# Perceiver block on one core: key rows before the latents, the key bias written by ScalarE, key-scale reciprocals on GpSimd

## The chip, the cores and the metric

The kernel runs on one core of a Trainium2 chip. The metric is the device time of one execution in microseconds. The engines of a core are TensorE (PE in the profile, its weight loads PEld), VectorE (DVE), ScalarE (ACT), GpSimd (POOL) and the DMA queue of SyncE (SP). Three runs of the kernel before took 455.82, 457.80 and 461.06 us, so its median is 457.8 us.

## The reference

Two layers are applied to `x` (2 x 128 x 256) with a context of 2 x 2048 rows of 256. What the change touches is the first layer's state-space block and the key half of the second layer's cross-attention:

```python
# layer 0, first part: multi-head latent attention, x += MLA(...)
# layer 0, second part (state-space block)
xz = x @ W_in.T ; xc = silu(conv(xp)) ; delta = softplus(dt @ W_dt.T + b_dt)
h = exp(delta*A[n]) * h + delta*B[n]*xc        # a scan over 128 positions, 16 states n
y = (sum_n h*C[n] + xc*Dp) * silu(z)           # the sum over n
# layer 1, cross-attention, from the context alone
k = ctx @ Wk + bk                              # 4096 rows x 256
s = max(abs(k), per row and head of 16)/127, at least 1e-8
kq = round(k / s) * s                          # 8-bit keys, one scale per row and head
v = ctx @ Wv + bv                              # per-channel scale from max(abs(v))
```

## The kernel before, in words

All loads, instructions and semaphores are written out by hand: each engine has its own program, run strictly in the order in which it is written, and a `wait_ge` on a semaphore holds everything behind it on that engine. One buffer `arena` holds most tiles at hand-set offsets; `w` in the trace is the tile `w1` with the state-space weights and, at its end, the key and value projection `w_kv` and its bias. `ps` is the eight accumulator banks.

The program has four stages that matter here.

**Latent attention (to about 78 us).** TensorE computes scores, turns the probabilities over (`prob_columns`, L1578), multiplies them with gathered latents (`weighted_latents`, L1591; `kvg` comes by nine DMAs) and projects them out (`attended`, L1598), once for each of the two batches b. In between stands `keys(0)` (L1633 and L1639), which needs `w1` to be loaded; SyncE issues that whole load after the nine gathers.

**State-space preparation (78 to 104 us).** Layer norm, projections, convolution, delta. VectorE's `first_input` (L1242) waits for the skip term's matmuls (`skip_read`).

**The loop (104 to 192 us).** Eight steps i, each with two of the sixteen states (s = 0, 1), interleaved with the key and value projection of 512 context rows per step. VectorE per step: two scans (L1251), two products with C (`read_out`, L1260), and for the keys two steps on `key_maxima` (L1150), the reciprocal of their scales (L1155) and `scaled_keys` (L1158), then `largest` of the values (L1187). GpSimd makes the scan inputs (L646) and the scales (L616). ScalarE makes decays (L906), evicts values (L830) and rounds the keys (`integers`, L838 and L841). TensorE per step: `key_columns` (L1659), `values_of` (L1648), the sums over states (L1748), `read_rows` (L1740), and `keys(i+3)`. Keys from step 1 on use only banks 2 and 3, so `keys(i+3)` waits until `scaled_keys(i+2)` has read them (`k_scaled`). The bias of the keys is the first matmul of each accumulation: a row of ones times the bias split into three bf16 parts (L1633), one for each bank.

**Values, feed-forward, queries, attention (from 192 us).** The 8-bit values are turned over (`value_rows`, L1836), the queries are made (L1822, L1335 to L1341), turned over (L1844) and masked by head (L691), and from 222 us VectorE reads scores (`maxima`, L1358), 32 units of four chunks, with `head_scales(h)` loading each head's key scales by DMA.

Of the kernel before, what the change touches and what calls it, by code (L numbers as in the profile page):

```python
# [14 lines left out]
P = 128  # L15
# [54 lines left out]
SUMS_PE = (0, 1, 2, 3, 4, 5, 6)  # L70
# [24 lines left out]
def perceiver_kernel(nc, x_d, seg_d, segrep_d, ctx_d, ctxT_d, rope_d, cst_d, w0a_d, w0q_d, w0b_d, w1_d, w2_d, w3_d, fill_d, out_d):  # L95
    with ExitStack() as ctx:
# [26 lines left out]
        neghalf = sb("neghalf", [P, B])  # L123
        spare = sb("spare", [P, 1])
# [95 lines left out]
        a_log = part(ET * DS).rearrange("p (t s) -> p t s", t=ET)  # L220
        w_kv = part(CH * 2 * D).rearrange("p (c n) -> p c n", c=CH)
# [41 lines left out]
        phase(2 * KEYS)  # L263
        vqb = take([CH, KEYS], BF16)
# [75 lines left out]
        (QLAT, WABS, MLAT, LAST_TAPS, DLAT, DLIN0, DLIN1, DBC, B_ROWS, Q_PS0, Q_PS1, Q_TR0, Q_TR1, ON_TR0, ON_TR1, VALUE0_MADE, Q_MADE,  # L340
# [16 lines left out]
        ld_w1 = sem("ld_w1")  # L357
        kvm_ready = sem("kvm_ready")
# [7 lines left out]
        k_scaled = sem("k_scaled")  # L366
        kmx_made = sem("kmx_made")
        ksc_made = sem("ksc_made")
        skip_read = sem("skip_read")
# [14 lines left out]
        qz_pool = sem("qz_pool")  # L384
        s_read = sem("s_read")
# [85 lines left out]
        rsum = sem("rsum")  # L471
# [30 lines left out]
        def _(sp):  # L502
# [21 lines left out]
            key_rows(1)  # L524
            sp.wait_ge(st_kv, 32)
# [3 lines left out]
            sp.dma_start(w1[:, :], w1_d).then_inc(ld_w1, 16)  # L529
# [44 lines left out]
        def _(pool):  # L574
# [3 lines left out]
            pool.wait_ge(half, 3)  # L578
# [20 lines left out]
            pool.wait_ge(ld_w1, 16)  # L599
# [49 lines left out]
            def sum_of(i):  # L649

                pool.wait_ge(hc_made, 2 * i + 2)
                pool.wait_ge(hc_used[1], i + 1)
                pool.tensor_tensor(th[:, :], th[:, :],
                                   hc[:, 1].rearrange("p t n -> p (t n)"), ALU.add).then_inc(hc_used[1], 1)

            pool.wait_ge(delta_ready, 2)
            pool.memset(th[:, :], 0.0).then_inc(hc_used[1], 1)
            pool.wait_ge(u_ready, 1)
            for i in range(NC - 1):
# [4 lines left out]
                if i not in SUMS_PE:  # L664
                    sum_of(i)
# [23 lines left out]
            for b in range(B):  # L689
                pool.wait_ge(qT_sb, b + 1)  # L690
                pool.tensor_scalar(qz[0][:, 0, b * L:(b + 1) * L], qT2[:, 0, b * L:(b + 1) * L], hmask[:, 0:1], None, ALU.mult)\  # L691
                    .then_inc(qz_pool, 1)
# [17 lines left out]
        def _(act):  # L710
# [103 lines left out]
            for b in range(B):  # L814
                act.activation(kvg[0:1, b * GB:(b + 1) * GB, :], bank(7, b * KVC, KVC, 0, 1).unsqueeze(1)
# [26 lines left out]

            def key_columns(i):
# [8 lines left out]
            key_columns(0)  # L852
            act.wait_ge(ld_w1, 16)
# [62 lines left out]
            for i in range(NC - 1):  # L916
# [3 lines left out]
                for m in range(CH):  # L920
                    values_of(i + 1, m)
                if i + 2 < NC:
# [114 lines left out]
        def _(dve):  # L1037
# [114 lines left out]
            def scaled_keys(i):  # L1152

                dve.wait_ge(ksc_made, i + 1)
# [975 lines left out]
```

## Time and profile before

| what | value |
|---|---|
| median of three runs | 457.8 us |
| the profiled execution's own time | 456.92 us |
| its span, first to last instruction | 454.7 us |
| busy: PE / DVE / ACT / POOL | 410.1 / 363.9 / 308.8 / 105.9 us |
| mean granted TensorE clock | 0.985 |

The profile shows one execution. Its time is 2.2 us above its span, which is what lies outside the first and last instruction. The longest chain of waits is made of TensorE for 43% and of VectorE for 35%. A busy share is a mean over stages: TensorE's 90% holds idle stretches, and in the loop it is close to 100%.

### The profile page before, as it was taken

The numbers are of one execution on the slowest core, as the hardware profiler recorded it, in microseconds if no ns is written. First come the engines' busy times: TensorE is split into PE (matmuls) and PEld (weight loads), VectorE is DVE, ScalarE is ACT, GpSimd is POOL, SyncE is SP. The second block draws the span as 40 slices with busy tenths as digits, with TensorE's granted clock in tenths as the row PEclk, the third lists the DMA queues.
The fourth block names the chain that finished last, engine by engine and source line by source line (L and its number), as shares of the span: only waits on it lengthen the run. The fifth ranks groups of instructions, "written<-read, shape, count | busy, mean of one in ns | idle before, by whom it ended". The sixth has DMA issues, their size and how long they took to land.

```text
span 454.7 us, 9348 instructions
## 1 busy us (share of the span) xinstructions
PE 410.1 (90%) x3814; PEld 308.5 (68%) x3854; DVE 363.9 (80%) x593; ACT 308.8 (68%) x394; POOL 105.9 (23%) x180
## 2 busy tenths in 40 slices
PE   8989889999999999799859889899888888888897
PEld 4778667865566554367527777777777777775586
DVE  2936643688999999888889999999999999955442
ACT  3256915579666667352888999999999999951120
POOL 4100030223555444000236333331111111100000
PEclk9999969999999999899989999999999999999999
DMA  7897920601100100079293554444444444000000
GB/s 273 291 398 250 189 119 1 255 3 46 25 23 27 32 14 0 0 255 438 106 368 140 196 219 190 190 187 186 187 186 186 187 188 186 3 1 0 2 0 23
DMA packets 13060, 63.32 MB, mean 139 GB/s; under 512 B 5946, under 2 KB 8666, under 8 KB 9562
## 3 DMA queue, kind: packets, MB, share of 16 engines
q1 hardware_dynamic: 12442, 59.19, 35.2%
q0 software_dynamic: 576, 3.54, 2.1%
q8 instruction: 30, 0.49, 0.4%
q14 instruction: 12, 0.10, 0.1%
HBM read 61.58 MB, written 1.15 MB: 138 GB/s over the span
## 4 chain that ended last, share of the span: by engine, by line
PE 43%; DVE 35%; issue 9%; DMA 7%; ACT 3%; SPq 2%; POOL 1%; DVEq 0%; POOLq 0%; ACTq 0%
DVE arena L1358 16%; DVE w L1358 8%; PE ps L1648 6%; PE ps L1748 6%; PE ps L1639 5%; DVE arena L1368 4%; PE ps L2014 3%; DMA w<-in_w 3%; PE ps L1534 2%; DMA arena<-in_segg 2%; PE ps L1688 2%; DMA arena<-ks_scr 2%; PE ps L2025 2%; DMA kv_scr<-arena 1%; PE ps L1890 1%
## 5 line engine op out<-in xcount | busy, mean ns | idle before, releaser
L1358 DVE CUSTOM_DVE_ANT_0 arena<-ps,arena 128x1024 f32<-128x1024 f32 x88 | 108.3, 1281 | 0.0
L1867 PE MATMUL ps<-arena 128*128 128x512 bf16 x216 | 68.2, 382 | 21.7 <-DVE arena L1358 18.5
L977 ACT ACTIVATE arena<-arena 128x4096 uint8<-128x4096 f32 x21 | 78.0, 3713 | 4.1 <-POOL arena L682 4.0
L1890 PEld LDWEIGHTS ps<-cst,arena 128*128 128x128 f32 x512 | 63.4, 141 | 24.8 <-issue 0.9
L1890 PE MATMUL ps<-cst,arena 128*128 128x128 f32 x512 | 77.3, 274 | 0.8 <-ACT arena L991 0.8
L1903 PE MATMUL ps<-vrow,arena 128*128 128x16 f16 x1024 | 59.7, 169 | 0.7 <-DVE arena L1368 0.6
L1903 PEld LDWEIGHTS ps<-vrow,arena 128*128 128x128 f16 x1024 | 53.2, 97 | 2.6 <-DVE arena L1368 1.3
L1358 DVE CUSTOM_DVE_ANT_0 w<-ps,arena 128x1024 f32<-128x1024 f32 x40 | 49.7, 1281 | 2.3 <-DMA arena<-ks_scr 2.3
L991 ACT ACTIVATE arena<-ps 128x512 f32<-128x512 f32 x91 | 47.4, 587 | 3.7 <-PE ps L1890 3.7
L1902 PE MATMUL ps<-vrow,arena 128*128 128x16 f16 x728 | 47.6, 170 | 0.2 <-ACT arena L991 0.2
L1902 PEld LDWEIGHTS ps<-vrow,arena 128*128 128x128 f16 x728 | 44.9, 96 | 0.3 <-ACT arena L991 0.3
L646 POOL TENSOR_TENSOR arena<-arena 128x1024 f32<-128x1024 f32 x14 | 33.0, 2361 | 40.2 <-DVE arena L1251 40.2
L678 POOL TENSOR_SCALAR arena<-arena 128x1 f32<-128x1 f32 x32 | 11.8, 369 | 121.3 <-DVE arena L1358 121.2
L977 ACT ACTIVATE arena<-w,arena 128x4096 uint8<-128x4096 f32 x10 | 37.1, 3714 | 2.0 <-POOL arena L682 2.0
L1251 DVE TENSOR_TENSOR_SCAN arena<-arena 128x1024 f32<-128x1024 f32 x16 | 37.2, 2363 | 0.2
L1748 PE MATMUL ps<-arena,cst 128*128 128x512 f32 x64 | 30.9, 624 | 2.5 <-DVE arena L1260 2.5
L906 ACT ACTIVATE arena<-arena 128x254 f32<-128x254 f32 x64 | 27.1, 495 | 5.8 <-DVE arena L1251 4.2
L1867 PEld LDWEIGHTS ps<-arena 128*128 128x128 bf16 x256 | 15.8, 96 | 22.3 <-issue 15.6
L1639 PE MATMUL ps<-w,arena 128*128 128x256 f32 x128 | 30.2, 379 | 0.0
L1648 PE MATMUL ps<-arena,w 128*128 128x512 f32 x64 | 29.4, 600 | 0.0
L1368 DVE TENSOR_SCALAR arena<-ps 128x1024 f16<-128x1024 f16 x37 | 25.4, 689 | 3.0 <-PE ps L1903 1.7
L1639 PEld LDWEIGHTS ps<-w,arena 128*128 128x128 f32 x128 | 24.3, 189 | 4.4 <-issue 0.3
(271 smaller groups left out, 694.5 us busy)
## 6 DMA issues: line engine op xcount, KB each, us to landing
arena<-ks_scr SPq DMA_DIRECT2D x16, 2048.0 KB, 7.6
arena<-in_w SPq DMA_DIRECT2D x1, 4488.0 KB, 17.3
arena<-in_columns SPq DMA_DIRECT2D x4, 1024.0 KB, 9.0
w<-in_w SPq DMA_DIRECT2D x1, 2927.0 KB, 12.9
arena<-in_w0b SPq DMA_DIRECT2D x1, 2560.0 KB, 18.5
arena<-in_w SPq DMA_DIRECT2D x1, 2048.0 KB, 7.9
arena<-in_fill SPq DMA_DIRECT2D x1, 2048.0 KB, 8.2
arena<-bc_scr SPq DMA_DIRECT2D x14, 128.0 KB, 3.1
```

Of the source, the lines that this page charges most:

```text
L977: act.activation(out8[:, :, 0], s_sb[u % 3], ACT.Exp, bias=nb[:, u % 3:u % 3 + 1], accum_out=zall[:, u:u + 1]).then_inc(p_ready, 1)
L991: act.activation(ptr[:, c, :].bitcast(F32), bank(4 + n % 3, 0, 512), ACT.Copy).then_inc(ptr_sb[1], 1)
L1251: dve.tensor_tensor_scan(hst[:, s, :], dA[:, s].rearrange("p t n -> p (t n)"), dbx[:, s].rearrange("p t n -> p (t n)"), 0.0, ALU.mult, ALU ...
L1358: dve.tensor_tensor_reduce(s_sb[slot][:, keys], ps[:, 2 * (c % 2):2 * (c % 2) + 2, :].rearrange("p a n -> p (a n)"), ksb[h % 2][:, keys], ...
L1368: dve.tensor_scalar(ptr[:, c, :], bank(4 + n % 3, 0, 512).bitcast(F16), -1024.0, None, ALU.add).then_inc(ptr_sb[0], 1)
L1639: mm = pe.matmul(bank(k_at + a, t * D, D), vT[:, c, i * CK + k:i * CK + k + P], w_kv[:, c, 0:D], start=False, stop=(c == CH - 1), skip_gro ...
L1648: mm = pe.matmul(bank(m, 0, CK), w_kv[:, c, D + m * P:D + (m + 1) * P], vT[:, c, i * CK:(i + 1) * CK], start=(c == 0), stop=(c == CH - 1))
L1748: mm = pe.matmul(bank(6 + n, 0, 512), ident, rows[:, n * 512:(n + 1) * 512], start=False, stop=True, skip_group_check=True)
L1867: mm = pe.matmul(bank(2 * (c % 2) + m, 0, 512), qz[h // 8][:, h % 8, b * L:(b + 1) * L], kT[:, h // 8, k:k + 512], start=True, stop=True)
L1890: mm = pe.transpose(bank(4 + n % 3, k * P, P), words[:, w:w + P], ident)
L1902: pe.matmul(bank(7, u * HW, HW), neg1024[:, :], vrow[:, h // 2, v:v + HW], start=False, stop=False)
L1903: mm = pe.matmul(bank(7, u * HW, HW), ptr[:, c, k * 2 * P + par:(k + 1) * 2 * P:2], vrow[:, h // 2, v:v + HW], start=(t == 0), stop=(t == ...
```

## The change

Eight edits, with no other line touched.

1. `w1` is loaded in two parts. The part from `w_kv` on goes first, ahead of the nine gathers, with its own semaphore `ld_wkv`. `keys(0)` moves on TensorE ahead of `weighted_latents(0)`, and on VectorE `key_maxima(0)` and `scaled_keys(0)` move ahead of the first residual. The row of means goes to bank 1 instead of 7.
2. `first_input` no longer waits for `skip_read`; the first `read_out` does.
3. From `keys(2)` on there is no bias matmul. ScalarE writes the bias into banks 2 and 3 (`key_bias`), after `k_scaled`, and TensorE waits for that (`bias_set`).
4. The reciprocals move from VectorE to GpSimd, as a power of -1 in one instruction behind each `scales_of` (`krs_made`).
5. VectorE reads `largest(i)` between `read_out(i, 1)` and `scaled_keys(i+2)`, no longer after it.
6. The clearing of `th` and its sum (two matmuls of zeros at the loop's end) go; 18 matmuls into an unused bank (`awake(18, 1)`) come before the last sums, once the values are evicted.
7. The integer values `vqb` lie in `w1`, so `head_scales(1)` is issued right behind `head_scales(0)`; VectorE's third unit waits for `vr_tr` instead.
8. On TensorE `value_rows(2)` and `query_columns(0)` come ahead of `queries(1)`, in place of `awake(2)`; head 0's masked queries are made by ScalarE (`q_first`), not GpSimd.

```diff
@@ SyncE
             key_rows(1)
+            sp.dma_start(w1[:, kv_at:W1], w1_d[:, kv_at:W1]).then_inc(ld_wkv, 16)
             sp.wait_ge(st_kv, 32)
...
-            sp.dma_start(w1[:, :], w1_d).then_inc(ld_w1, 16)
+            sp.dma_start(w1[:, 0:kv_at], w1_d[:, 0:kv_at]).then_inc(ld_w1, 16)
...
             head_scales(0)
+            head_scales(1)
             sp.wait_ge(vq_ready, 4)
             sp.dma_start(w3b, w3_d[:, w3a:W3]).then_inc(ld_w3b, 16)
-            sp.wait_ge(vr_tr, 8)
-            head_scales(1)
@@ GpSimd, scales_of(i)
                     .then_inc(ksc_made, 1)
+                pool.wait_ge(ksc_made, i + 1)
+                if i:
+                    pool.wait_ge(k_scaled, i)
+                pool.tensor_tensor(krs[:, :], ksc[:, i * CT * H:(i + 1) * CT * H], negone[:, :], ALU.pow).then_inc(krs_made, 1)
...
-            pool.memset(th[:, :], 0.0).then_inc(hc_used[1], 1)
@@ ScalarE
+            def key_bias(i):
+                act.wait_ge(k_scaled, i)
+                act.activation(ps[:, 2:4, :].rearrange("p a (t d) -> p (a t) d", d=D),
+                               b_k[:, :].unsqueeze(1).broadcast_to([P, CT, D]), ACT.Copy).then_inc(bias_set, 1)
...
                 for m in range(CH):
                     values_of(i + 1, m)
+                if i + 3 < NC:
+                    key_bias(i + 3)
                 if i + 2 < NC:
                     integers(i + 2)
...
             def query_columns(b):
                 act.wait_ge(pe_step, (Q_TR0, Q_TR1)[b])
+                act.activation(qz[0][:, 0, b * L:(b + 1) * L], bank((4, 7)[b], 0, L // 2).bitcast(BF16), ACT.Identity,
+                               scale=hmask[:, 0:1]).then_inc(q_first, 1)
@@ VectorE
             def scaled_keys(i):
-                dve.wait_ge(ksc_made, i + 1)
-                link(dve.reciprocal(krs[:, :], ksc[:, i * CT * H:(i + 1) * CT * H]))
+                dve.wait_ge(krs_made, i + 1)
...
-            dve.wait_ge(skip_read, 1)
             dve.wait_ge(z_gate, 1)
...
                 read_out(i, 1)
+                largest(i)
                 if i + 2 < NC:
                     scaled_keys(i + 2)
-                largest(i)
@@ TensorE
             def keys(i):
                 if i > 1:
-                    pe.wait_ge(k_scaled, i)
+                    pe.wait_ge(bias_set, i - 1)
...
-                    pe.matmul(bank(k_at + a, 0, 2 * D), selb[0:S3, 0:1].broadcast_to([S3, P]), ...
+                    if i < 2:
+                        pe.matmul(bank(k_at + a, 0, 2 * D), selb[0:S3, 0:1].broadcast_to([S3, P]), ...
...
-            pe.wait_ge(hc_used[1], NC)
-            sum_of(NC - 2, 1, th)
-            first_sum(NC - 1)
+            pe.wait_ge(v_sb, CH * NC)
+            awake(18, 1)
+            sum_of(NC - 1, 0)
...
             columns(3, 1)
-            awake(2, 0)
+            value_rows(2)
+            query_columns(0)
             queries(1)
-            query_columns(0)
-            value_rows(2)
```

On VectorE, step 0 of the loop and the scans of step 1, before. Here `ps` is the banks and `arena` everything in the big buffer; the instruction named SCALAR_TENSOR_TENSOR on L1251 is the scan.

```order
L1260 TENSOR_TENSOR arena<-arena,ps 128x1024 [waits c_ps,h_ready]
L1150 TENSOR_REDUCE arena<-ps 128x64 [waits ksc_made,k_ps]
L1260 TENSOR_TENSOR arena<-arena,ps 128x1024 [waits c_ps,h_ready]
L1155 RECIPROCAL arena<-arena 128x64 [waits ksc_made]
L1158 TENSOR_TENSOR arena<-ps,arena 128x1024 [waits kint_ready,dve_chain]
L1187 TENSOR_REDUCE arena<-arena 128x2 [waits v_sb]
L1251 SCALAR_TENSOR_TENSOR arena<-arena 128x1024 [waits dbx_ready,dA_ready,hc_made] x2
```

The same place in the change; L1266 is `read_out`, L1156 `key_maxima`, L1192 `largest`, L1163 `scaled_keys`.

```order
L1266 TENSOR_TENSOR arena<-arena,ps 128x1024 [waits c_ps,skip_read,h_ready]
L1156 TENSOR_REDUCE arena<-ps 128x64 [waits ksc_made,k_ps]
L1266 TENSOR_TENSOR arena<-arena,ps 128x1024 [waits c_ps,h_ready]
L1192 TENSOR_REDUCE arena<-arena 128x2 [waits v_sb]
L1163 TENSOR_TENSOR arena<-ps,arena 128x1024 [waits kint_ready,krs_made]
L1255 SCALAR_TENSOR_TENSOR arena<-arena 128x1024 [waits dbx_ready,dA_ready,hc_made] x2
```

The reciprocal has gone from the row, and `largest` stands between the second `read_out` and `scaled_keys`.

On GpSimd, one step of the loop in the change. L654 is a scan input, L620 the scales, and L625, which before has no counterpart, the power.

```order
L654 TENSOR_TENSOR arena<-arena 128x1024 [waits h_ready,ld_b0]
L620 TENSOR_SCALAR arena<-arena 128x64 [waits kmx_made]
L625 TENSOR_TENSOR arena<-arena,negone 128x64 [waits k_scaled,ksc_made]
L654 TENSOR_TENSOR arena<-arena 128x1024 [waits h_ready,ld_b1]
```

The power stands between the two scan inputs of the step, so the second of them starts later by its length.

On TensorE, the end of the latent attention's first half, in the change. L1586 is `prob_columns`, L1643 and L1649 `keys(0)`, L1599 `weighted_latents`, L1606 `attended(0)`.

```order
L1586 MATMUL ps<-cst,vrow 73x128 [waits pt_sb,probs]
L1586 MATMUL ps<-cst,vrow 73x128 x3
L1643 MATMUL ps<-arena,selb 128x512 [waits ld_wkv,bk3_ready,wvo_sb]
L1649 MATMUL ps<-w,arena 128x256 x4
L1643 MATMUL ps<-arena,selb 128x512
L1649 MATMUL ps<-w,arena 128x256 x4
L1599 MATMUL ps<-arena 64x64 [waits kvm_ready,pt_sb,ld_kvg]
L1599 MATMUL ps<-arena 64x64 x15
L1599 MATMUL ps<-arena 64x64 [waits kvm_ready,pt_sb]
L1599 MATMUL ps<-arena 64x64 x15
L1606 MATMUL ps<-arena 128x256 [waits ot_sb]
L1606 MATMUL ps<-arena 128x256 x7
```

Before, the four rows of `keys(0)` stood behind those of `attended(0)`, with waits for `ld_w1` and `kvm_ready` besides.

## Rows read from the trace of the kernel before

**Rows 1.** Windows: start:end, length, busy us of PE, PEld, DVE, ACT, POOL, clock, DMA

```profile
58.00:65.00 7.00, 6.74 (x16) 5.02 (x16) 2.43 (x5) 0.10 (x1) 2.50 (x5) 0.55 0.25 104
234.00:400.00 166.00, 148.34 (x2354) 124.97 (x2393) 164.18 (x273) 159.32 (x151) 41.62 (x107) 0.99 0.45 177
```

**Rows 2.** Timeline, 53 to 84 us: start, us, engine, line, tiles, idle before

```profile
55.20 2.09 PE L1591 MATMUL ps<-arena 73*64 73x64 f32 x64 [1.08 <-DMA arena<-kv_scr]
...
58.15 6.74 PE L1598 MATMUL ps<-arena 128*128 128x256 f32 x16 [0.87 <-ACT arena L808]
...
62.16 0.39 POOL L601 CAST arena<-w 96x256 bf16<-96x256 f32 x1 [48.87 <-DMA w<-in_w]
...
65.66 0.38 PE L1633 MATMUL ps<-arena,selb 96*128 96x512 bf16 x1 [0.77 <-POOL arena L610]
...
69.55 1.04 PE L1578 MATMUL ps<-cst,vrow 128*73 128x128 f32 x8
...
74.75 3.72 PE L1598 MATMUL ps<-arena 128*128 128x256 f32 x16 [0.70 <-ACT arena L808]
```

**Rows 3.** Timeline, preparation and the loop's first VectorE work

```profile
86.93 4.15 DVE L1197 SCALAR_TENSOR_TENSOR arena<-arena,w 128x256 f32<-128x256 f32 x9 [0.72 <-ACT arena L862]
...
101.31 1.30 DVE L1234 TENSOR_TENSOR arena<-arena 128x1024 f32<-128x1024 f32 x1
...
104.58 1.22 DVE L1242 TENSOR_TENSOR arena<-arena,ps 128x1024 f32<-128x1024 f32 x1 [1.97 <-PE ps L1730]
```

**Rows 4.** The chain of waits: keys(3), both halves, and keys(7)

```profile
117.55 1.73 PE ps L1639 x8
119.49 1.73 PE ps L1639 x8
...
163.47 1.73 PE ps L1639 x8
```

**Rows 5.** Timeline, step 3 of the loop, VectorE and ScalarE

```profile
144.53 1.22 DVE L1150 TENSOR_REDUCE arena<-ps 128x64 f32<-128x1024 f32 x1
145.66 1.21 DVE L1260 TENSOR_TENSOR arena<-arena,ps 128x1024 f32<-128x1024 f32 x1
146.79 0.55 DVE L1155 RECIPROCAL arena<-arena 128x64 f32<-128x64 f32 x1
147.37 1.23 DVE L1158 TENSOR_TENSOR arena<-ps,arena 128x1024 f32<-128x1024 f32 x1
...
149.31 1.15 ACT L838 ACTIVATE arena<-arena,cst 128x1024 f32<-128x1024 f32 x1
...
149.64 4.46 DVE L1251 TENSOR_TENSOR_SCAN arena<-arena 128x1024 f32<-128x1024 f32 x2
```

**Rows 6.** Groups of POOL instructions over the whole span, busy us and mean ns

```profile
L678 POOL TENSOR_SCALAR arena<-arena 128x1 f32<-128x1 f32 x32 | 11.8, 369 | 121.3 <-DVE arena L1358 121.2
...
L583 POOL TENSOR_TENSOR ln_rs<-ln_ve,neghalf 128x1 f32<-128x1 f32 x12 | 6.7, 557 | 71.7 <-DVE ln_ve L1057 71.7
L616 POOL TENSOR_SCALAR arena<-arena 128x64 f32<-128x64 f32 x8 | 3.5, 435 | 6.3 <-DVE arena L1150 6.3
```

**Rows 7.** The chain of waits at the loop's end and behind it

```profile
182.20 0.23 PE ps L1740 x2
...
187.08 3.68 PE ps L1748 x4
190.76 1.72 PE ps L1780 x4
...
198.05 1.08 PE ps L1463 x5
```

**Rows 8.** Timeline, from the second query projection to the third attention unit

```profile
219.06 1.13 PE L1822 MATMUL ps<-arena,xnT 128*128 128x256 f32 x4 [0.46 <-ACT xnT L716]
...
219.28 0.29 DVE L1341 TENSOR_SCALAR arena<-arena 128x256 bf16<-128x256 f32 x1
...
234.30 1.28 DVE L1358 CUSTOM_DVE_ANT_0 w<-ps,arena 128x1024 f32<-128x1024 f32 x1 [2.26 <-DMA arena<-ks_scr]
```

More of the change, by code:

```diff
@@ L69 @@
 LAST = UNITS - 1
-SUMS_PE = (0, 1, 2, 3, 4, 5, 6)
 def on_vector(u, c):
@@ L262, in perceiver_kernel @@
         ksT = take([NC // 2, P])
-        phase(2 * KEYS)
-        vqb = take([CH, KEYS], BF16)
+        vqb = w1[:, 0:KEYS].bitcast(BF16).rearrange("p (c k) -> p c k", c=CH)
         w_f1 = w2[:, 0:CH * FF].rearrange("p (c n) -> p c n", c=CH)
@@ L687, in query_columns @@
                     .then_inc(qz_pool, 1)
[L689 to L692, printed above, removed]
+            pool.wait_ge(qT_sb, B)
             query_columns(1)
@@ L852, in _ @@
             key_columns(0)
+            act.wait_ge(ld_wkv, 16)
             act.wait_ge(ld_w1, 16)
@@ L897, in _ @@
                 act.activation(th[:, m * 512:(m + 1) * 512], th[:, m * 512:(m + 1) * 512], ACT.Ln, bias=1.0).then_inc(sp_ln, 1)
+            key_bias(2)
             act.wait_ge(aneg_ready, 1)
@@ L1162, in attended @@
                 if b == 0:
+                    key_maxima(0)
+                    scaled_keys(0)
+                else:
                     dve.wait_ge(ld_w1, 16)
@@ L1165, in attended @@
                     dve.tensor_scalar(taps, taps, 0.5, None, ALU.mult).then_inc(conv_half, 1)
-                else:
-                    key_maxima(0)
-                    scaled_keys(0)
                 dve.wait_ge(mla_out, b + 1)
@@ L1351, in maxima @@
                 if c == 0:
+                    if u == 2:
+                        dve.wait_ge(vr_tr, 8)
                     if u >= 3:
@@ L1629, in keys @@
                 if i > 1:
-                    pe.wait_ge(k_scaled, i)
+                    pe.wait_ge(bias_set, i - 1)
                 k_at = 2 if i else 6
                 for a in range(2):
-                    pe.matmul(bank(k_at + a, 0, 2 * D), selb[0:S3, 0:1].broadcast_to([S3, P]),
-                              bk3[0:S3, :].unsqueeze(1).broadcast_to([S3, 2, D]),
-                              start=True, stop=False, skip_group_check=True)
+                    if i < 2:
+                        pe.matmul(bank(k_at + a, 0, 2 * D), selb[0:S3, 0:1].broadcast_to([S3, P]),
+                                  bk3[0:S3, :].unsqueeze(1).broadcast_to([S3, 2, D]),
+                                  start=True, stop=False, skip_group_check=True)
                     for t in range(2):
@@ L1661, in key_columns @@
                 mm.then_inc(kt_ps, 1)
+            pe.wait_ge(wvo_sb, 3)
+            pe.wait_ge(bk3_ready, 2)
+            pe.wait_ge(ld_wkv, 16)
+            keys(0)
             pe.wait_ge(ld_kvg, 16 * WIN)
@@ L1666, in _ @@
             attended(0)
-            pe.wait_ge(wvo_sb, 3)
-            pe.wait_ge(kvm_ready, B)
-            pe.wait_ge(bk3_ready, 2)
-            pe.wait_ge(ld_w1, 16)
-            keys(0)
             for n in range(4, 8):
@@ L1742, in read_rows, with sum_of @@
                 mm.then_inc(c_ps, 1)
-            def sum_of(i, s, rows):
+            def sum_of(i, s):
                 pe.wait_ge(hc_made, 2 * i + s + 1)
+                rows = hc[:, s].rearrange("p t n -> p (t n)")
                 for n in range(2):
@@ L1861, in scores @@
                 if c == 0:
-                    pe.wait_ge(qz_pool, u + 1 if h == 0 else h + 2)
+                    if h == 0:
+                        pe.wait_ge(q_first, u + 1)
+                    else:
+                        pe.wait_ge(qz_pool, h)
                 if n >= 2:
```

41 lines of the change are left out of this document (20 added, 21 removed).

## The prediction

> **What bounds the kernel now.** I read the windows first, for each engine's load and TensorE's clock by stage. From 234 to 400 us VectorE is busy 164.2 of 166 us [rows 1]: that stage is VectorE's, the change doesn't touch it, and what is won ahead of it comes out whole. Between 58 and 65 us TensorE has a mean clock of 0.55 [rows 1], its lower level of 1.2 GHz for nearly all of the stretch.
>
> The timeline of that place shows why keys(0) matters. At 55.20 TensorE has stood idle for 1.08 us, so it had been free since 54.12; then come the latents, and attended(0), which takes 6.74 us at the low clock against 3.72 for attended(1) at the full one. The key projection's weights come with the large load and are used by GpSimd only at 62.16. keys(0) runs from 65.66 to 69.55, 3.89 us, and everything behind it waits [rows 2].
>
> In the loop I read the chain of waits. keys(3) starts at 117.55 behind its bias matmul and keys(7) at 163.47, four steps, so 11.48 us a step [rows 4], and the chain is TensorE throughout. VectorE's own step is shorter: from key_maxima to the next scan 5.11 us, two scans 4.46, one more read_out about 1.1 [rows 5], 10.7 in all. So the reciprocal's 0.58 us (146.79 to 147.37 [rows 5]) is hidden by TensorE now; what the move buys is decided by TensorE's new step.
>
> **The sum, edit by edit**, against the profiled execution's 456.92 us, which is 0.9 below the median of 457.8.
>
> *keys(0) early.* TensorE is free at 54.12. GpSimd's splitting of the bias takes from 62.16 to just before 65.66, 3.3 us [rows 2]; it now waits for a load of 656 KB (1,282 of 5,854 words a partition) that is issued ahead of the gathers, and for scores that TensorE has finished before it turns the first probabilities over, near 48 us, so it is over by 52. keys(0) then runs to 58.0. From the start of the latents to attended(0) it is 58.15 - 55.20 = 2.95, so attended(0) starts at 61.0. Its clock is the first choice: the idle spell ahead of 58 us is filled now, so I take 3.72 us, to 64.7. What follows took from 69.55 to 78.47 (74.75 + 3.72), 8.92 us [rows 2], and now ends at 73.6. Gain 4.85. If attended(0) stays at the low clock the gain is 1.85. The nine gathers may come up to 2.8 us later than 55.20 at no cost, since keys(0) covers them.
>
> *first_input.* VectorE waited 1.97 us for the skip term and is ready at 102.61 [rows 3]. It starts there. ScalarE's first key_bias falls in its wait for VectorE's delta ahead of the first decay, which hides it.
>
> *Bias by ScalarE.* keys(3) is now reached over VectorE and ScalarE. From first_input to the end of scaled_keys(2) VectorE took 12.1 us (104.58 to 116.7); less 0.58 for the reciprocal, and 1.13 more for largest, which now stands ahead. From 102.61 that gives 115.3. Then the bias: no row writes banks from ScalarE. Its ends are 0.6 us (a pass over 512 columns) and 2.3 (twice the 1.15 of L838, 128 x 1024 [rows 5]); I take 1.15, the row of the same shape. keys(3) starts at 116.6, 0.55 ahead of its old bias matmul at 117.2. From there TensorE binds again, each block of keys shorter by its two bias matmuls, 119.49 - 117.55 - 1.73 = 0.21 each [rows 4]: five blocks, 2.1 us. TensorE leaves the last step 2.6 us earlier. The wait for scaled_keys and bias is then hidden, since VectorE's step with largest moved up is 10.1 us and TensorE's 11.05; at 2.3 us of bias the loss is 0.9.
>
> *The loop's end.* TensorE's last transposes begin at 182.43 (182.20 + 0.23) and end at 182.9 [rows 7]; now at 180.3. The sum of zeros goes. The 18 matmuls cost 1.08/5 = 0.22 us each [rows 7], 3.9 together, to 184.2; they hold back the last sums, whose inputs are there at about 184, by next to nothing, and keep the clock: the four passes from 187.08 took 3.68 where the four from 190.76 took 1.72 [rows 7]. The sums end at 184.2 + 1.7 + 1.7 = 187.6 instead of 192.5. Gain up to here 4.9 us, in which first_input, the bias, the zeros and the clock all lie. The values' scale is ready before that, so nothing else takes over.
>
> *Queries.* query_columns(0) needs the integers that VectorE has at 219.57 (219.28 + 0.29), and takes some 0.28; queries(1), at 219.06 before [rows 8], now stands behind it and starts at 219.85. Loss 0.8. ScalarE's two masked pieces, about 0.3 us each, keep pace with that.
>
> *head_scales(1).* The third unit's wait of 2.26 us for that load [rows 8] goes, since the load is issued some 24 us earlier; w3 behind it is needed only after 400 us. vr_tr is complete by then. Gain 2.26.
>
> *The power on GpSimd*, the unknown. Below lies the trace's 0.43 us for one pass over 128 x 64 (L616 [rows 6]). Above: a power of one element per partition takes 0.557, a plain operation of one element 0.369; the excess of 0.19 for each of the 64 elements would be 12 us [rows 6]. The nearest row by shape and engine is L616; with the excess once it is 0.6, and I take 1 us. The Trainium skill's "GPSIMD Engine Reference", section 7, says that a chain of dependent fp32 operations costs 4 cycles for each link unless the loop is unrolled, which speaks for the upper end; no run here shows how this loop is built. In the loop the scales are done some 1.85 us behind the start of key_maxima (1.22 for it, 0.2 to hand over, 0.43 [rows 5, 6]), and scaled_keys comes 3.4 us behind it (key_maxima, read_out and largest at 1.13 each), so up to 1.55 us is free, and up to 2.5 costs under 1.3. Where scaled_keys(1) runs, VectorE idled 0.72 ahead of the convolution [rows 3] and loses the reciprocal, so 1.25 is free; beyond that each us is lost once.
>
> Sum: 4.85 + 4.9 - 0.8 + 2.26 = 11.2, to **445.7, say 446 us**.
>
> **Rivals.**
> *The power is slow.* Then key_maxima, scales, power, scaled_keys, bias and keys form a ring that decides the step: 1.2 + 0.4 + X + 1.2 + 1.2 + 3.5, and five hand-overs of 0.1 to 0.2, some 8.4 + X. From X = 2.6 us it passes TensorE's 11.05, and from there each us costs 1 us in each of six steps and one in the preparation. With X = 3 the execution takes about 452, with 3.5 455, with 4 459, with 5 466, with 6 473, and with 12 over 510. It decides at X = 3.8: above that the kernel is slower than before. For it: a power of a single element takes a fifth of a us longer than a plain operation, so there is much work per element. Against it: the excess may be the length of a pipelined body and be paid once. Chance 0.37, of which 0.10 between 3.2 and 4.5 us (within 1%), 0.27 above.
> *Smaller gain ahead of 80 us.* attended(0) stays at 1.2 GHz, since the dip may come from the spells before 54 us; or the early load delays the gathers by more than keys(0) covers. 449 us. Chance 0.10.
> *The bias takes the place of what it removes:* ScalarE's write costs nearer 3 us than 1, and the step grows to about 12 us. 452 us or more. Chance 0.03.
> *The reciprocals' move does nothing*, since VectorE isn't the bound: in my sum it is worth under 0.6 us, with largest moved up as its price. It is part of the forecast, not against it.
> The forecast itself has 0.50.
>
> **Numbers.** The forecast's own range is 443.5 to 448.5: the power up to 2.5 us and the bias up to 2.3 pull it up by 2.6, a scan of the last step that took 1.4 us longer than its like may not do so again, and the loss of 0.8 may be hidden. The slow power holds more than 2 in 10, so the range must reach into it: up to 467, X of about 5.1, which leaves 0.2 above. About 1% is what runs of this kernel tell from no change: from 453.2 to 462.4. Faster 0.63 (the forecast, the two small rivals); same 0.10; slower 0.27.
>
> **What the profile after would show.** The row of GpSimd's power, 128 x 64: at most 1.5 us if I am right, and then no wait of VectorE's scaled_keys for it. keys(0) starting near 54 us, attended(0) of 3.7 us, the second residual near 73.7. The distance between keys blocks 11.05, TensorE without idle time from the second step on. The last sums at full clock, 1.7 us for four passes, behind 3.9 us of idle matmuls. No wait for key scales at unit 3, but integer_queries(1) 0.8 later behind integer_queries(0). If instead VectorE waits for GpSimd in every step and TensorE for the bias, it is the slow power; if ScalarE's bias row is 3 us, the third rival. A gathered latent landing after 58 us, or a load for keys(0) after 52, would make the first term wrong.

## The result, and the profile after

The changed kernel takes **521.86 us** (median of 4 runs, 520.09 to 524.40) against 457.88 us (455.82 to 461.06, 4 runs) of the kernel before: a ratio of 1.1395, 95% interval 1.1308 to 1.1481. It is slower by 64 us, where the forecast was faster by 11, and lies 55 us above the upper end of the range (467 us). The profiled execution took 520.54 us, its span is 518.4, and TensorE's mean granted clock fell from 0.985 to 0.947.

The page's groups (busy time, mean ns of one, idle time just before and what ended most of it) name the cause in one row, and in three rows of those who wait for it:

```profile
L625 POOL TENSOR_TENSOR arena<-arena,negone 128x64 f32<-128x64 f32 x8 | 84.6, 10576 | 0.7
...
L1649 PE MATMUL ps<-w,arena 128*128 128x256 f32 x128 | 40.8, 485 | 38.8 <-ACT ps L840 38.8
L1163 DVE TENSOR_TENSOR arena<-ps,arena 128x1024 f32<-128x1024 f32 x8 | 9.8, 1225 | 76.5 <-POOL arena L625 76.5
...
L840 ACT ACTIVATE ps<-w 128x1024 f32<-128x1024 f32 x6 | 6.1, 1024 | 45.2 <-DVE arena L1163 45.2
```

L625 is GpSimd's power. One takes 10.576 us, where the rows that stood next to it before showed 0.43 and 0.557 [rows 6]. Behind it stands a row of waits: VectorE's `scaled_keys` (L1163) for the power, 76.5 us in eight instances; ScalarE's bias write (L840) for `scaled_keys`; TensorE's keys (L1649) for the bias. In the chain of waits the power alone has 16% of the span; by engine the chain is:

```profile
DVE 39%; PE 22%; POOL 20%; issue 12%; ACT 4%; DMA 1%; SPq 0%; DVEq 0%; POOLq 0%; ACTq 0%
```

**The start.** TensorE does what was predicted for it. In its timeline (start, duration) keys(0) starts at 53.77, ahead of the latents, and attended(0) takes 3.72 us instead of 6.74 [rows 2], because the clock is up (granted 1.00 from 58 to 65 us, before 0.55 [rows 1]):

```profile
53.77 0.38 PE L1643 MATMUL ps<-arena,selb 96*128 96x512 bf16 x1
...
60.53 3.72 PE L1606 MATMUL ps<-arena 128*128 128x256 f32 x16 [0.70 <-ACT arena L802]
```

VectorE gives half of it back. `scaled_keys(0)` now stands ahead of the first residual and waits 11.37 us for the power, and the second residual (L1175) comes at 75.97, against 78.50 before and 73.7 predicted:

```profile
72.48 1.23 DVE L1163 TENSOR_TENSOR arena<-ps,arena 128x1024 f32<-128x1024 f32 x1 [11.37 <-POOL arena L625]
73.63 0.41 DVE L1175 TENSOR_TENSOR xres<-ps,xres 128x256 f32<-128x256 f32 x1
...
75.97 0.42 DVE L1175 TENSOR_TENSOR xres<-ps,xres 128x256 f32<-128x256 f32 x1
```

**A step of the loop** on VectorE, where 11.48 us a step stood before [rows 4]:

```profile
131.94 1.23 DVE L1163 TENSOR_TENSOR arena<-ps,arena 128x1024 f32<-128x1024 f32 x1 [9.13 <-POOL arena L625]
133.08 5.47 DVE L1255 TENSOR_TENSOR_SCAN arena<-arena 128x1024 f32<-128x1024 f32 x2
138.47 1.19 DVE L1266 TENSOR_TENSOR arena<-arena,ps 128x1024 f32<-128x1024 f32 x1
140.62 1.23 DVE L1156 TENSOR_REDUCE arena<-ps 128x64 f32<-128x1024 f32 x1 [0.95 <-PE ps L1649]
141.76 1.21 DVE L1266 TENSOR_TENSOR arena<-arena,ps 128x1024 f32<-128x1024 f32 x1
142.89 1.22 DVE L1192 TENSOR_REDUCE arena<-arena 128x2 f32<-128x1024 f32 x1
153.05 1.23 DVE L1163 TENSOR_TENSOR arena<-ps,arena 128x1024 f32<-128x1024 f32 x1 [8.95 <-POOL arena L625]
```

From one `scaled_keys` to the next it is 21.1 us here and 20.8 on average over the four steps from 131.94 to 215.05. This is the ring of the first rival: `key_maxima` (L1156), the power, `scaled_keys`, bias, keys. Two rows are longer than before. The two scans (L1255), which that ring doesn't hold, take 5.47 us instead of 4.46 [rows 5]. TensorE's block of keys takes 6.30 instead of about 3.5: the engine had stood still for 9.92 us and its clock is down (granted 0.61 from 131 to 142 us):

```profile
134.28 6.30 PE L1649 MATMUL ps<-w,arena 128*128 128x256 f32 x16 [9.92 <-ACT ps L840]
```

Behind the loop the sum is as forecast: from the output projection's first matmul to the end it is 518.4 - 257.76 = 260.6 us, against 454.7 - 192.5 = 262.2 before; a gain of 1.6 where the prediction's two terms there (2.26 won by `head_scales(1)`, 0.8 lost to the queries) make 1.5.

### The profile page after: what moved, and what is told of

Read it like the earlier page. It is cut to its first block, busy times and chain, and to the rows that moved or that the text cites. A ratio compares the mean times of both kernels' runs of the same rounds, so it can differ in the third digit from the quotient of the medians.

```text
span 518.4 us, 9402 instructions
## 1 busy us (share of the span) xinstructions
PE 424.8 (82%) x3854; PEld 314.9 (61%) x3854; DVE 365.8 (71%) x585; ACT 314.3 (61%) x402; POOL 190.5 (37%) x186
## 3 DMA queue, kind: packets, MB, share of 16 engines
HBM read 61.58 MB, written 1.15 MB: 121 GB/s over the span
## 4 chain that ended last, share of the span: by engine, by line
DVE 39%; PE 22%; POOL 20%; issue 12%; ACT 4%; DMA 1%; SPq 0%; DVEq 0%; POOLq 0%; ACTq 0%
POOL arena L625 16%; DVE arena L1366 15%; DVE w L1366 7%; DVE arena L1255 4%; DVE arena L1376 4%; PE ps L2022 3%; POOL arena L654 3%; PE ps L1471 2%; PE ps L1542 2%; DMA arena<-in_segg 1%; PE ps L2033 1%; PE ps L1658 1%; PE ps L1566 1%; PE ps L1898 1%; PE ps L1759 1%
## 5 line engine op out<-in xcount | busy, mean ns | idle before, releaser
L1875 PE MATMUL ps<-arena 128*128 128x512 bf16 x256 | 75.9, 377 | 15.1 <-DVE arena L1366 14.9
L625 POOL TENSOR_TENSOR arena<-arena,negone 128x64 f32<-128x64 f32 x8 | 84.6, 10576 | 0.7
L1649 PE MATMUL ps<-w,arena 128*128 128x256 f32 x128 | 40.8, 485 | 38.8 <-ACT ps L840 38.8
L1163 DVE TENSOR_TENSOR arena<-ps,arena 128x1024 f32<-128x1024 f32 x8 | 9.8, 1225 | 76.5 <-POOL arena L625 76.5
L1649 PEld LDWEIGHTS ps<-w,arena 128*128 128x128 f32 x128 | 31.8, 253 | 46.9 <-ACT ps L840 40.2
L654 POOL TENSOR_TENSOR arena<-arena 128x1024 f32<-128x1024 f32 x14 | 32.9, 2353 | 32.8 <-DVE arena L1255 32.8
L1255 DVE TENSOR_TENSOR_SCAN arena<-arena 128x1024 f32<-128x1024 f32 x16 | 43.2, 2736 | 0.2
L840 ACT ACTIVATE ps<-w 128x1024 f32<-128x1024 f32 x6 | 6.1, 1024 | 45.2 <-DVE arena L1163 45.2
L1658 PE MATMUL ps<-arena,w 128*128 128x512 f32 x64 | 32.1, 645 | 0.0
L587 POOL TENSOR_TENSOR ln_rs<-ln_ve,neghalf 128x1 f32<-128x1 f32 x12 | 6.6, 551 | 66.4 <-DVE ln_ve L1063 66.4
```

What stands on the lines that cost most here:

```text
L625: pool.tensor_tensor(krs[:, :], ksc[:, i * CT * H:(i + 1) * CT * H], negone[:, :], ALU.pow).then_inc(krs_made, 1)
L654: pool.tensor_tensor(dbx[:, s], u[:, :, :], bcb[:, n % 4, :].unsqueeze(1).broadcast_to([P, ET, T]), ALU.mult)\
L1255: dve.tensor_tensor_scan(hst[:, s, :], dA[:, s].rearrange("p t n -> p (t n)"), dbx[:, s].rearrange("p t n -> p (t n)"), 0.0, ALU.mult, ALU ...
L1649: mm = pe.matmul(bank(k_at + a, t * D, D), vT[:, c, i * CK + k:i * CK + k + P], w_kv[:, c, 0:D], start=False, stop=(c == CH - 1), skip_gro ...
L1658: mm = pe.matmul(bank(m, 0, CK), w_kv[:, c, D + m * P:D + (m + 1) * P], vT[:, c, i * CK:(i + 1) * CK], start=(c == 0), stop=(c == CH - 1))
L1875: mm = pe.matmul(bank(2 * (c % 2) + m, 0, 512), qz[h // 8][:, h % 8, b * L:(b + 1) * L], kT[:, h // 8, k:k + 512], start=True, stop=True)
```

## Experiments

`ratio` is against the kernel before, run beside it on the same chip (its median is 456.0 to 458.8 us there), so it is the fairer measure between kernels. The last two columns are from the profiled execution.

| kernel | median us (lowest to highest) | ratio, 95% interval | loop step us | span us |
|---|---|---|---|---|
| before | 457.88 (455.82 to 461.06) | | 11.48 | 454.7 |
| changed | 521.86 (520.09 to 524.40) | 1.1395, 1.1308 to 1.1481 | 20.8 | 518.4 |
| r_dve | 446.76 (445.86 to 447.97) | 0.972, 0.9673 to 0.9767 | 11.05 | 445.8 |
| r_dve_last | 444.75 (444.59 to 446.41) | 0.9695, 0.9646 to 0.9743 | 11.05 | 442.5 |
| pow8 | 449.70 (448.29 to 450.81) | 0.9792, 0.974 to 0.9844 | 11.3 | 447.1 |
| pow32 | 478.83 (478.05 to 480.06) | 1.0434, 1.0383 to 1.0484 | 15.1 | 476.0 |
| before_pow | 530.66 (529.05 to 533.35) | 1.1625, 1.1558 to 1.1691 | 20.3 | 529.1 |
| awake_loop | 519.02 (518.45 to 521.37) | 1.1377, 1.1315 to 1.1439 | 20.2 | 517.2 |
| no_act_bias | 447.42 (446.57 to 450.31) | 0.9813, 0.9769 to 0.9857 | 11.48 | 444.5 |
| no_awake | 448.13 (446.22 to 449.50) | 0.9806, 0.9765 to 0.9847 | 11.05 | 447.5 |
| keys0_late | 448.49 (447.12 to 449.16) | 0.9813, 0.9786 to 0.984 | 11.05 | 446.6 |
| q_old | 444.55 (443.69 to 447.29) | 0.9738, 0.9711 to 0.9764 | 11.05 | 445.1 |
| r_dve_last_again | 446.06 (444.57 to 448.43) | 0.9759, 0.9724 to 0.9794 | 11.05 | 444.1 |
| warm_end | 444.11 (443.52 to 444.38) | 0.9714, 0.9689 to 0.9738 | 11.05 | 442.0 |

**The power taken out** (`r_dve`), all else of the change kept:

```diff
-                pool.tensor_tensor(krs[:, :], ksc[:, i * CT * H:(i + 1) * CT * H], negone[:, :], ALU.pow).then_inc(krs_made, 1)
+                link(dve.reciprocal(krs[:, :], ksc[:, i * CT * H:(i + 1) * CT * H]))     # VectorE, in scaled_keys
```

> The change with the reciprocals back on VectorE (no power), largest still ahead of scaled_keys. Theory A (the 10.6 us power sets the ring of the loop and nothing else is wrong): about 446 us, keys blocks 11.05 us apart, no wait of scaled_keys. Rival B (the power is only part; the other edits, ScalarE's bias above all, cost time too): over 458 us.

446.76 us: 75.1 us less than the changed kernel, and 2.8% faster than before. The forecast of 446 us was thus met by this kernel, in which nothing waits for a power. Its steps stand in this trace too: second residual 73.43 (predicted 73.7), keys(3) at 112.10 (116.6 less the 4.85 of the start is 111.75), steps of 11.05.

**`largest` back behind `scaled_keys` as well** (`r_dve_last`):

```diff
-                largest(i)
                 if i + 2 < NC:
                     scaled_keys(i + 2)
+                largest(i)
```

> As r_dve, but scaled_keys ahead of largest again. Theory A: largest in between has no use without the power and costs the first key block 0.6 to 1.1 us, so 445.5 us, 0.5 below r_dve. Rival B: as r_dve. If largest in between were free, both are equal.

keys(3) starts at 110.47 instead of 112.10, and the first maxima at 212.47 instead of 214.09. Of these 1.6 us, 0.5 is already there at the start of the loop (first `read_out` at 104.18 and 104.67), ahead of anything that this edit touches, and 1.1, one pass of VectorE, is the move. So reading the largest values in between costs 1.1 us and hides nothing, once the power is gone. The ratios of the two kernels (0.972 and 0.9695) don't tell them apart.

**The power on 8 and on 32 of the 64 columns**, VectorE's reciprocal on the rest (`pow8`, `pow32`):

```diff
+                pool.tensor_tensor(krs[:, 0:8], ksc[:, i * CT * H:i * CT * H + 8], negone[:, 0:8], ALU.pow).then_inc(krs_made, 1)
+                link(dve.reciprocal(krs[:, 8:CT * H], ksc[:, i * CT * H + 8:(i + 1) * CT * H]))
```

> The change, but GpSimd's power makes only 8 of the 64 reciprocals and VectorE the other 56. Theory A: the power's length grows by 0.16 us for each element, (10.57 - 0.55)/63, so 0.55 + 7 x 0.16 = 1.7 us, which hides: 446 us, as r_dve. Rival C (the power has a large fixed cost at more than one element): a power row of many us and over 460 us.

> The change, but GpSimd's power makes 32 of the 64 reciprocals. Theory A: power row 0.55 + 31 x 0.16 = 5.5 us; ring 8.4 + 5.5 = 13.9 us a step against 11.05; 446 plus 6 steps of 2.9 and about 4 in the preparation: 467 to 470 us if TensorE keeps its clock, up to 480 if it falls to 1.2 GHz in the keys blocks. Rival C: near the changed kernel's 522 us.

The power's own instances, by line (min/median/max ns), first 8 columns, then 32, then the changed kernel's 64:

```profile
L625 POOL TENSOR_TENSOR arena<-arena,negone x8: 1659/1662/1685, 61.9 to 164.2; 128x8 f32<-128x8 f32 x8
```
```profile
L625 POOL TENSOR_TENSOR arena<-arena,negone x8: 5448/5450/5472, 61.6 to 189.3; 128x32 f32<-128x32 f32 x8
```
```profile
L625 POOL TENSOR_TENSOR arena<-arena,negone x8: 10571/10572/10594, 61.9 to 225.0; 128x64 f32<-128x64 f32 x8
```

With the 0.55 us of one column these four lie on a line: (1.66 - 0.55)/7, (5.45 - 0.55)/31 and (10.57 - 0.55)/63 are each 0.158 to 0.159 us for a column. So the excess of a power is paid for every element of a partition, not once. (The power of one column has the exponent -0.5, the others -1; the three widths of -1 give the same slope by themselves, 0.158 and 0.160 us.) With 32 columns the step is 15.07 us where the ring's 8.4 + 5.45 gives 13.9, and with 64 it is 20.8 where it gives 19.0; this remainder is taken up below.

`pow8` misses its expectation of 446 us. Its power takes 1.66 us, hardly more than the 1.55 that the prediction called free, VectorE never waits for it in the loop, and yet the first maxima come 2.9 us later than in `r_dve` (217.00 against 214.09). What is held up is GpSimd's next scan input (L654, L650), which stands behind the power. First `r_dve`, then `pow8`, the same step:

```profile
128.82 2.36 POOL L650 TENSOR_TENSOR arena<-arena 128x1024 f32<-128x1024 f32 x1
...
132.10 4.46 DVE L1252 TENSOR_TENSOR_SCAN arena<-arena 128x1024 f32<-128x1024 f32 x2
```
```profile
131.94 2.36 POOL L654 TENSOR_TENSOR arena<-arena 128x1024 f32<-128x1024 f32 x1
...
133.41 5.21 DVE L1257 TENSOR_TENSOR_SCAN arena<-arena 128x1024 f32<-128x1024 f32 x2
```

In `pow8` the scan input ends at 134.30, 0.89 us into the two scans, and they take 0.75 us longer. VectorE's step in `r_dve` is 10.6 us where TensorE doesn't hold it (scans at 110.90, 121.50 and 132.10); 0.75 more, less 0.05 for the shorter reciprocal, is the 11.3 of `pow8`, with VectorE never idle. So a power that nobody waits for still made VectorE the bound of the loop.

**The power alone in the kernel before** (`before_pow`): the power and `negone` added to GpSimd, the reciprocal and no other line changed.

```diff
+                pool.tensor_tensor(krs[:, :], ksc[:, i * CT * H:(i + 1) * CT * H], negone[:, :], ALU.pow).then_inc(krs_made, 1)
-                link(dve.reciprocal(krs[:, :], ksc[:, i * CT * H:(i + 1) * CT * H]))
```

> The kernel before with one edit: the reciprocal of the 64 key scales is made by GpSimd's power instead of by VectorE. Theory A, the power alone is the cause (10.57 us each, waited for each time): the second residual comes some 4 to 5 us later, the preparation loses about 9.3 us, and each of the six steps of the loop goes from 11.48 to 19.5 to 21 us (the bias is two matmuls here and the largest value still stands behind the scaling, so one pass less is ahead of the power's end), some 8 to 9.5 us each: about 457.8 + 4.5 + 9.3 + 53 = 525 us, 515 to 535. Theory B, the power hurts only because of how it meets the other edits (the bias by ScalarE, the largest value read in between, keys(0) early): then this kernel stays below 490 us.

530.66 us, inside the expected range. The power costs 74.6 us in the kernel before (ratio 1.1625 of 456.03) and 75.1 in the changed one: it needs no help from the other edits, and they bring 10.5 us with it (1.1625 against 1.1395) and 12 without (0.972). Within the total one part lay off: from the second residual to the first scan it lost 15.2 us (82.67 to 125.32, before 78.50 to 105.90), not 9.3. VectorE's timeline of a step, where `largest` (L1193) follows `scaled_keys`:

```profile
165.06 1.23 DVE L1164 TENSOR_TENSOR arena<-ps,arena 128x1024 f32<-128x1024 f32 x1 [10.21 <-POOL arena L624]
166.21 1.21 DVE L1193 TENSOR_REDUCE arena<-arena 128x2 f32<-128x1024 f32 x1
...
167.33 4.46 DVE L1257 TENSOR_TENSOR_SCAN arena<-arena 128x1024 f32<-128x1024 f32 x2
```

The scans take 4.46 us here, not 5.47. GpSimd's product with two inputs of 128 x 1024, the scan input, was over when they began:

```profile
165.00 2.36 POOL L653 TENSOR_TENSOR arena<-arena 128x1024 f32<-128x1024 f32 x1
```
In the changed kernel, where `largest` isn't in between, the same product reaches into the first scan (next experiment).

**TensorE kept busy while it waits** (`awake_loop`), the changed kernel with

```diff
                 if i + 3 < NC:
+                    pe.wait_ge(v_sb, CH * (i + 2))
+                    awake(32, 1)
                     keys(i + 3)
```

> The changed kernel with 32 idle matmuls of 512 columns (some 6.9 us at full clock) ahead of each of the five keys blocks of the loop, where TensorE stands idle while VectorE waits for the power. It tests where the step of 20.8 us comes from beyond 8.4 + 10.57 = 19.0. Theory A, the rest is TensorE's clock, which falls in the idle time and makes a keys block take 5.7 to 6.3 us instead of 3.46: with the idle matmuls a block takes about 3.5 to 4 us and the step is near 18.6 us, so the kernel is 10 to 12 us faster than the changed one, about 511 us. Theory B, the blocks are slow for another reason (waiting for their inputs) or the idle matmuls end too late: no gain, 521 us or up to 5 more.

The clock is held (granted 1.00 from 131 to 142 us, in the changed kernel 0.61), and the blocks are as short as in `r_dve` (3.62 to 3.72 us):

```profile
136.19 3.72 PE L1649 MATMUL ps<-w,arena 128*128 128x256 f32 x16 [3.01 <-ACT ps L840]
```

But the step falls only from 20.8 to 20.2 us, and the kernel's ratio (1.1377) isn't told apart from the changed one's (1.1395). The expectation of 10 to 12 us fell: it took the whole remainder for the clock. GpSimd's and VectorE's rows show what binds then:

```profile
133.79 2.35 POOL L654 TENSOR_TENSOR arena<-arena 128x1024 f32<-128x1024 f32 x1
```
```profile
133.86 1.22 DVE L1163 TENSOR_TENSOR arena<-ps,arena 128x1024 f32<-128x1024 f32 x1 [9.13 <-POOL arena L625]
135.00 5.47 DVE L1255 TENSOR_TENSOR_SCAN arena<-arena 128x1024 f32<-128x1024 f32 x2
140.39 1.19 DVE L1266 TENSOR_TENSOR arena<-arena,ps 128x1024 f32<-128x1024 f32 x1
141.50 1.21 DVE L1156 TENSOR_REDUCE arena<-ps 128x64 f32<-128x1024 f32 x1
```

VectorE never idles between `scaled_keys` and `key_maxima` (L1156), so the ring now closes over VectorE's own queue: 7.64 us from the one to the other, and 12.56 on to the next `scaled_keys`, 20.2. The scans stretched by 1.0 us lie in that path. GpSimd's product was held up behind the power, starts with `scaled_keys` and ends at 136.14, 1.14 us into the scan. Without the stretch the first leg would be 6.6 us, and `before_pow` shows just that: 7.76 us from `scaled_keys` to `key_maxima` (165.06 to 172.82), of which `largest` is 1.12. So of the 1.8 us by which a step exceeds the rival's formula, about 1.0 is the product running into the scan, and 0.6 the clock on top of it: in the changed kernel VectorE waits 0.37 to 0.95 us for the keys ahead of `key_maxima`. The last 0.2 is the leg itself: the formula took 6.4 us for it, by ScalarE and TensorE, where VectorE's own queue needs 6.6. `pow32` agrees: 7.6 + 2.0 + 5.45 = 15.0, measured 15.07, and its steps with a block of keys of 3.72 us and of 5.41 us differ by less than 0.1.

**Single terms of the forecast**, each undone in `r_dve_last`.

The bias by two matmuls again (`no_act_bias`; ScalarE's writes of the bias are gone too):

```diff
-                    pe.wait_ge(bias_set, i - 1)
+                    pe.wait_ge(k_scaled, i)
-                    if i < 2:
+                    if True:
```

> The version with the reciprocal on VectorE and the largest value behind the scaling as before (444.75 us), with the keys' bias of the loop made by two matmuls again instead of ScalarE's write into the banks. Prediction's step: 0.43 us of TensorE for each of five blocks, in a loop that TensorE bounds, 2.1 us slower, 446.9 us, with steps of 11.48 instead of 11.05. Rival: ScalarE's write is itself on the path (about 1 us behind the scaling), so that the matmuls, which wait for nothing but the scaling, cost no more: within 0.5 us of 444.75, steps near 11.05 to 11.2.

The first matmuls of two blocks lie 144.93 - 133.44 = 11.49 us apart, in `r_dve_last` 143.71 - 132.67 = 11.04. The first maxima move by 1.9 us (214.33 against 212.47) and the span by 2.0. The step held.

No idle matmuls before the last sums (`no_awake`):

```diff
-            pe.wait_ge(v_sb, CH * NC)
-            awake(18, 1)
```

> The version with the reciprocal on VectorE and the largest value behind the scaling as before (444.75 us), without the 18 idle matmuls ahead of the last sums and without their wait for the values. If these keep the clock: the eight last sums and what follows fall back to the low clock, in the kernel before four passes took 3.68 us instead of 1.72, so 1 to 3 us slower, 446 to 448 us. If they only take room: TensorE reaches the last sums sooner and the kernel is 0 to 1.5 us faster. The prediction's step counted the clock as worth about 2 us.

TensorE's timeline, first without, then with them:

```profile
178.74 3.78 PE L1756 MATMUL ps<-arena,cst 128*128 128x512 f32 x4 [4.23 <-DVE arena L1263]
182.31 3.02 PE L1781 MATMUL ps<-arena,cst 128*128 128x512 f32 x4
```
```profile
173.93 4.05 PE L1468 MATMUL ps<-identb 128*128 128x512 bf16 x18
178.32 1.98 PE L1756 MATMUL ps<-arena,cst 128*128 128x512 f32 x4 [0.34 <-DVE arena L1263]
180.14 1.88 PE L1783 MATMUL ps<-arena,cst 128*128 128x512 f32 x4
```

Eight passes take 6.4 us instead of 3.7, and the first maxima come 3.25 us later, of which 0.4 was there before the loop. The prediction had four of these passes at half speed, 3.68 against 1.72 us, so about 2 us; the 2.7 here are the same mechanism in all eight.

keys(0) behind attended(0) again, its load still early (`keys0_late`; the same four lines go from ahead of the latents):

```diff
             attended(0)
+            pe.wait_ge(wvo_sb, 3)
+            pe.wait_ge(bk3_ready, 2)
+            pe.wait_ge(ld_wkv, 16)
+            keys(0)
```

> The version with the reciprocal on VectorE and the largest value behind the scaling as before (444.75 us), with keys(0) behind attended(0) again; its weights are still loaded early. The prediction took 4.85 us for the move, of which 3.0 are attended(0) at full clock instead of at the low one and 1.85 the place of keys(0) in otherwise idle time. If that holds, attended(0) takes 6.7 us again and the kernel is 4 to 5 us slower, about 449.3 us. If the clock doesn't hang on keys(0), attended(0) stays near 3.7 us and the loss is 1 to 2 us, about 446.5. If the later steps had slack there (VectorE's own work ahead of the second residual), there is no loss.

Neither expectation is met whole. attended(0) takes 5.13 us, between the two levels:

```profile
57.51 5.13 PE L1603 MATMUL ps<-arena 128*128 128x256 f32 x16 [0.87 <-ACT arena L798]
```

The second residual comes at 75.33 against 72.94, and the first maxima 2.4 us later. So the place is worth 2.4 us, 1.4 of it by the clock (5.13 against 3.72). The kernel before has the second residual at 78.50, 3.2 us later than this one, which moves keys(0) back but keeps the early load. Of these 3.2, 0.9 is the wait for GpSimd's split of the bias, which is gone (keys(0) follows attended(0) at once, at 62.48); 0.6 is an earlier start of attended(0), and 1.6 its shorter time, 5.13 instead of 6.74. That the early load brought the last two isn't shown: there is one profiled execution of each kernel. The prediction gave load and place one figure, 4.85.

The queries' old order (`q_old`: `awake(2, 0)`, two idle matmuls, then `queries(1)`, `query_columns(0)`, `value_rows(2)` again):

> The version with the reciprocal on VectorE and the largest value behind the scaling as before (444.75 us), with the order of the queries on TensorE as in the kernel before (second projection ahead of the first turning, two idle matmuls ahead of it). The prediction charged the new order 0.8 us, and the changed kernel showed 0.64 us from integer queries to maxima: 0.6 to 0.8 us faster, 444.1 us, if that delay reaches the end; no change if the first unit waited for something else of the new order that comes earlier by it (the first block of queries turned sooner).

From the first integer queries to the first maxima it is 211.67 - 206.90 = 4.77 us instead of 212.47 - 207.07 = 5.40: the 0.63 is real up to there. Yet this execution's span is longer, 445.1 us, and the ratios don't decide between the two.

**Where that went: the experts' stage.** From the first maxima to the end it is 230.0 us in `r_dve_last`, `pow8`, `no_act_bias` and the changed kernel (230.2), 231.7 in `r_dve`, `no_awake` and `keys0_late`, and 233.4 in `q_old`. Nearly all of it lies in the first 40 matmuls of the experts: 8.88 us in the first group, 10.57 in the second, and in `q_old` 11.82:

```profile
416.04 11.82 PE L2020 MATMUL ps<-xnT,arena 128*128 128x256 f32 x40
```

Ahead of them TensorE stands idle several times for 0.35 to 1.5 us. `warm_end` is `q_old` with 15 idle matmuls in these gaps:

```diff
             self_columns(0)
+            awake(7, 4)
             self_out(0)
...
             self_columns(1)
+            awake(2, 2)
             self_out(1)
-            awake(5)
+            awake(7)
             columns(5, 0)
+            awake(2)
...
             columns(5, 1)
+            awake(2)
```

> The version with the queries in their old order (reciprocal on VectorE), with 15 more idle matmuls in the last 40 us, each where TensorE stands idle for 0.35 to 1.5 us. In the profiled executions of some versions the first 40 matmuls of the experts' stage took 11.8 us, at the low clock, and in others 8.9. If idle time ahead of them sets that, they take 8.9 us now, the stretch from the first maxima to the end is 230.1 us and the kernel takes 441 to 442 us by its profile, some 1 to 3 us below the version with the largest value behind the scaling. If it is chance, the stretch is 230 to 233.5 us as before and nothing is won; if the idle matmuls hold back what follows them, up to 1 us is lost.

> The same kernel as the version with the reciprocal on VectorE and the largest value behind the scaling, once more, to stand beside the one with a warm end on the same chip: 444 to 447 us, and in the profile 230 or 231.7 us from the first maxima to the end.

```profile
415.84 8.88 PE L2024 MATMUL ps<-xnT,arena 128*128 128x256 f32 x40
```

From 398 to 416 us TensorE is now busy 17.28 us instead of 14.12 in `r_dve_last_again`, and from 416 to 426 its granted clock is 1.00 instead of 0.83. But `r_dve_last`, the same kernel as `r_dve_last_again`, had 1.00 there too, behind the same 14.12 us: the low clock in that stage comes in some executions and not in others. `warm_end` takes 444.11 us with all six runs within 0.9 us (443.52 to 444.38); the other, on the same chip, 446.06 with six runs over 3.9 us. It is 2.9% below the kernel before, but its ratio (0.9714) isn't told apart from those of `r_dve_last`, `q_old` and `r_dve_last_again`. The smaller scatter is what the idle matmuls would bring if they keep that clock up; six runs of each, and one profiled, make it likely and don't prove it.

## Why the prediction was wrong

**The failed step is the term "the power on GpSimd", taken as 1 us.** It measured 10.57. The two ends stood in the prediction, 0.43 and 12 us, and the choice between them was made by the row nearest in shape (L616, a plain operation over 128 x 64). The row nearest in kind was the power of one column [rows 6]: its excess of 0.19 us over a plain operation of one column can't be told from a cost per instruction by that row alone, and the prediction took it so. Multiplied by 64 it gave 12 us, 14% off. The upper end was close to the truth, and the lower one told nothing of this operation. The Trainium skill's "GPSIMD Engine Reference", section 7, which puts a price per element on a dependent fp32 chain, pointed to that end. Its section 4.1, which has GpSimd about twice as slow as VectorE in two-input work, speaks of add, multiply and max, and its factor can't be carried over to this power: `r_dve`'s reciprocal over 128 x 64 takes 0.54 us and the power 19 times that.

**A second step failed, what the power does to others while nobody waits for it.** The prediction had up to 1.55 us free and up to 2.5 cost under 1.3. `pow8`, with 1.66 us, costs 2.9, since the second scan input starts later by the power's length and runs beside the scans. That later start was noted with the order of GpSimd's instructions, and the sum gave it no price.

**The rival's mechanism is what happened, and its formula fell short.** With X = 10.57 its own slope (473 us at X = 6, 7 us more per us) gives 505; measured 521.9. The start loses 2.5 us more than `r_dve` (75.97 against 73.43), which the prediction hadn't counted; the preparation 11.0 instead of 9.3; each of six steps 1.8 more, by the stretched scans, the fallen clock and VectorE's own queue, which the ring didn't hold; and the 18 idle matmuls start so late (250.26) that they hold the last sums back by 1.6. Added to 505 that is 521.6.

**The other steps held**, as `r_dve` shows: start 73.43 (73.7), steps 11.05, first maxima 214.09 (222.30 - 4.85 - 4.9 + 0.8 = 213.35), 446.76 us (445.7). From the second residual to the first input it is 24.20 us instead of 26.08, so 1.9 of the 1.97 for the skip term's wait came. The power cost 75 us, the rest won 11 to 12. ScalarE's bias took 1.03 us (1.15 predicted) and the third rival didn't come; `largest` in between costs 1.1 us as charged. That moving the reciprocal does nothing for the loop fits `r_dve`, which has it on VectorE and still steps by TensorE's 11.05; no run has it moved at a low price. At the start the size held (5.1 us in `r_dve`, 4.85 predicted), and its parts are only in part known (`keys0_late`).

**The chances.** The slow power had 0.27 and the range ended at X of about 5.1. With two ends 28 times apart and no row against the upper one, more weight and a wider range belonged there.

## What to carry to other kernels

A function evaluated element by element is priced by the same function on another size, with its excess multiplied by the number of elements, before it is priced by another operation of the same shape. Before work is moved off an engine that isn't the bound, ask who then waits for the receiver: a reciprocal of 0.58 us hidden under TensorE became 10.57 us that every step of the loop waited for. Ask too what stands behind the new instruction on its engine, and what that will then run beside: in `pow8` this alone cost 3 us. And a wait that lets TensorE idle can cost twice, once itself and once in the clock of what follows; here the second part was 0.6 us of a step of 20.8.

## What the runs showed of the hardware

- GpSimd's fp32 power costs 0.158 to 0.159 us for each element of a partition: 0.55, 1.66, 5.45 and 10.57 us for 1, 8, 32 and 64 of them over 128 partitions (the first with exponent -0.5, the others with -1).
- A VectorE scan with two inputs of 128 x 1024 is stretched by nearly as long as a two-input product of GpSimd runs beside it: two scans took 4.46 us without overlap, 5.21 with 0.89 us of it (`pow8`) and 5.47 with 1.14 (`awake_loop`); GpSimd's product took 2.35 us either way. The Trainium skill's "GPSIMD Engine Reference", section 1, has the two engines share their SBUF interfaces and contend when VectorE reads two SBUF inputs; the trace agrees.
- In the changed kernel TensorE, after 7.2 to 9.9 us of idle time, ran a block of keys in 5.7 to 6.3 us, at a mean granted clock of 0.58 to 0.64, so mostly at the 1.2 GHz level. It took 3.7 us at 2.4 GHz in `awake_loop`, where 7 us of idle matmuls stood in the gap, although 2 to 3 us of idle time remained.
- ScalarE wrote 128 x 1024 fp32 into two banks in 1.03 us.
